# Edge loops of a graph attention kernel: the sum of gathered rows in two pieces, VectorE's steps in another order, GpSimd's turn signals out

## The chip, the cores and the metric

The kernel runs on one core of a Trainium2 chip. The metric is the device time of one launch in microseconds (us). TensorE (PE in the profile), VectorE (DVE), ScalarE (ACT), GpSimd (POOL) and SyncE (SP) run side by side, each through its own list of instructions, and order themselves by semaphores.

## What is computed

One layer of a graph transformer on 625 nodes of 768 features: two graph attention layers (GATv2) over 10,625 edges, a linear attention mixer, and a mixture of experts. The change touches the edge part of both attention layers:

```python
def gatv2(x, src, dst, Ws, bs, Wd, bd, attn):
    H, D = attn.shape                       # 8 x 96 in the first layer, 1 x 768 in the second
    fs = (x @ Ws + bs).reshape(-1, H, D)
    fd = (x @ Wd + bd).reshape(-1, H, D)
    e = leaky_relu(fs[src] + fd[dst], 0.2)
    logits = einsum('ehd,hd->eh', e, attn)
    m = segment_max(logits, dst)
    ex = exp(logits - m[dst])
    alpha = ex / segment_sum(ex, dst)[dst]
    return elu(segment_sum(alpha[:, :, None] * fs[src], dst))
```

The kernel writes the leaky relu as 0.2 z + 0.8 relu(z). The part 0.2 z is linear, so its product with `attn` is worked out once for each node and carried along in the last columns of the gathered rows (8 more columns in layer 1, one more in layer 2). What is left for each edge is the sum of two rows, max(z, 0) times the scaled attention vector, and a sum over each head.

## The kernel before

The edges lie in 84 tiles of 128 (one edge to a partition). Each of two loops ("loop 1", "loop 2") goes over the 84 tiles. A ring of G = 5 slots holds gathered rows. In the words used below:

- GpSimd issues three indirect transfers a step: the **source gather** (L577, rows of `table_src` into `ring_s`), the **target gather** (L583, rows of `table_dst` into `ring_d`) and the **scatter** (L588, the logits of a tile into a dense table). Step t waits until the logits of tile t are there (`edge_done`), gathers tile t+5 into the slot that came free, and scatters tile t. The three stand in one queue, in this order, and the first five tiles are gathered ahead of the loop. A step's scatter also waits for the scatter six tiles back.
- VectorE, in loop 1, does for tile t the **sum** of the two gathered rows (L1026, 776 columns, waits for both gathers), the **one-hot** rows of the tile ahead (L1033, used by TensorE to count edges in L1533), the **product** with the attention vector (L1038, 768 columns, both inputs in SBUF), the **head sums** (L1042) and the **total** (L1047, 8 columns, which signals `edge_done`). In the code the total of tile t-1 stands ahead of the sum of tile t; that is the place right behind its own head sums.
- In loop 2 the one head's sum is taken by the product itself (L1068, whose second input lies in PSUM), so there are only sum (769 columns), product and total (L1073). From tile 67 on, steps of other work (`project`) are mixed in: divisions, weights, transposed tiles, and the results of the products that TensorE runs at the end of the loop.
- `turn` (L1017) lets VectorE wait, ahead of the total of tile t-1, for a signal `edge_turn` that GpSimd gives in front of the gathers of step t-3.

Loop 1 is followed by a load of the dense table and the softmax (`dense(0)`), loop 2 by `dense(1)`; both wait for the last tiles, in loop 2 by way of the `project` steps.

Of the kernel before, what the change touches and what calls it, by code (L numbers as in the profile page):

```python
# [17 lines left out]
ALU = mybir.AluOpType  # L18
# [15 lines left out]
ET = -(-EDGES // EP)  # L34
FULL = EDGES // EP
SPREAD = 12
G = 5
# [12 lines left out]
DE_SLOTS = 8  # L50
PROJ_STEPS = 5 + 3 * T
PROJ_FROM = ET - PROJ_STEPS + 3
TURN_LAG = 3
TREE = N // 2
BL = CAP // 128

# [11 lines left out]
def build(nc, x, src, dst, W1s, b1s, W1d, b1d, attn1, ln1_w, ln1_b, Wos, bos, Wod, bod, attno, lno_w,  # L68
          lno_b, qkv_wT, qk_bcols, v_brow, proj_wT, proj_b, proj_matT, gate_wT, gate_bias, moe_w, out):
    ctx = ExitStack()  # L70
    with ctx:
        def sem(name):
            return ctx.enter_context(nc.semaphore(name))
# [10 lines left out]
        def dram(name, shape, dt=F32):  # L84
# [3 lines left out]
        WL = [DX, D + 1]  # L88
# [109 lines left out]
        ring_s, ring_d, hot_s, hot_d = zone([  # L198
            ("ring_s", [EP, G, DX], F32), ("ring_d", [EP, G, DX], F32),
            ("hot_s", [EP, G, TP], F16), ("hot_d", [EP, G, TP], F16)])  # L200
# [49 lines left out]
        z_ready, mul_ready = [sem(f"z_ready{l}") for l in range(2)], [sem(f"mul_ready{l}") for l in range(2)]  # L250
        sum_ready = sem("sum_ready")
        edge_done = [sem(f"edge_done{l}") for l in range(2)]
        edge_turn = [sem(f"edge_turn{l}") for l in range(2)]
        scattered = [sem(f"scattered{w}") for w in range(W)]
        hot_square, hot_d_ready = sem("hot_square"), sem("hot_d_ready")
        hot_ready, hot_used, counts_ready = sem("hot_ready"), sem("hot_used"), sem("counts_ready")
# [296 lines left out]
        def _(pool):  # L553
# [19 lines left out]
            def edges(l):  # L573

                def gather_src(t):
                    j = t % G
                    pool.indirect_dma_start(  # L577
                        out=ring_s[:, j, 0:WL[l]], out_offset=None, in_=table_src[l],
                        in_offset=bass.IndirectOffsetOnAxis(ap=src_i[:, t:t + 1], axis=0)).then_inc(gathered[j], 16)

                def gather_dst(t):
                    j = t % G
                    pool.indirect_dma_start(  # L583
                        out=ring_d[:, j, 0:WL[l]], out_offset=None, in_=table_dst[l],
                        in_offset=bass.IndirectOffsetOnAxis(ap=dst_i[:, t:t + 1], axis=0)).then_inc(gathered[j], 16)

                def scatter(t):
                    pool.indirect_dma_start(  # L588
                        out=dense_logits[l], out_offset=bass.IndirectOffsetOnAxis(ap=cell_i[:, t:t + 1], axis=0),
                        in_=logits[:, t, 0:HL[l]], in_offset=None).then_inc(scattered[t % W], 16)  # L590

                pool.wait_ge(idx_ready, 1)
                pool.wait_ge(src_written[l], TABLE)
                pool.wait_ge(mm_used, 20 * l + 15)
                for t in range(G):
                    gather_src(t)
                pool.wait_ge(mm_used, 20 * l + 20)
                pool.wait_ge(dst_written[l], TABLE + 16)
                for t in range(G):
                    gather_dst(t)  # L600
                pool.wait_ge(filled[l], 16)
                for t in range(ET):
                    pool.wait_ge(edge_done[l], t + 1)
                    if t + G < ET:
                        pool.sem_inc(edge_turn[l], 1)
                        gather_src(t + G)
                        gather_dst(t + G)
                    if t >= W:
                        pool.wait_ge(scattered[t % W], scatters(l, t - W))
                    scatter(t)  # L610
# [288 lines left out]
        def _(dve):  # L899
# [114 lines left out]
                dve.wait_ge(ext_ready, (2 * l + 2) * T)  # L1014
                dve.tensor_scalar((rows[:, 2, :], att_ps)[l], rows[:, 2, :], 0.8, None, ALU.mult).then_inc(att_scaled, 1)

            def turn(l, t):  # L1017

                if TURN_LAG <= t < ET - G + TURN_LAG:
                    dve.wait_ge(edge_turn[l], t - TURN_LAG + 1)  # L1020

            def edge_sum(l, t):

                j = t % G
                dve.wait_ge(gathered[j], gathers(l, t))
                dve.tensor_tensor(ring_s[:, j, 0:WL[l]], ring_s[:, j, 0:WL[l]], ring_d[:, j, 0:WL[l]], ALU.add).then_inc(z_ready[l], 1)  # L1026

            def edges_first():

                def hot(t):  # L1030
                    if t >= G:
                        dve.wait_ge(hot_used, t - G + 1)
                    dve.tensor_scalar(hot_s[:, t % G, :], iota_h[:, :], src_f[:, t:t + 1], None, ALU.is_equal).then_inc(hot_ready, 1)  # L1033

                def weigh(t):
                    dve.wait_ge(z_ready[0], t + 1)
                    v = ring_s[:, t % G, 0:D]
                    dve.scalar_tensor_tensor(out=v, in0=v, scalar=0.0, in1=rows[:, 2, :], op0=ALU.max, op1=ALU.mult).then_inc(mul_ready[0], 1)  # L1038

                def heads(t):  # L1040
                    dve.wait_ge(mul_ready[0], t + 1)
                    dve.tensor_reduce(head_sum[:, t % 2, :], ring_s[:, t % G, 0:D].rearrange("p (h d) -> p h d", h=HEADS1),  # L1042
                                      AX.X, ALU.add).then_inc(sum_ready, 1)

                def total(t):
                    dve.wait_ge(sum_ready, t + 1)
                    dve.tensor_tensor(logits[:, t, :], head_sum[:, t % 2, :], ring_s[:, t % G, D:DX], ALU.add).then_inc(edge_done[0], 1)  # L1047

                scale_attention(0)
                hot(0)  # L1050
                dve.wait_ge(att_scaled, 1)
                for t in range(ET):
                    turn(0, t)
                    if t >= 1:
                        total(t - 1)
                    edge_sum(0, t)
                    if t + 1 < ET:
                        hot(t + 1)
                    weigh(t)
                    heads(t)  # L1060
                total(ET - 1)

            def edges_second():

                def weigh(t):
                    dve.wait_ge(z_ready[1], t + 1)
                    j = t % G
                    dve.scalar_tensor_tensor(out=ring_d[:, j, 0:D], in0=ring_s[:, j, 0:D], scalar=0.0, in1=att_ps,  # L1068
                                             op0=ALU.max, op1=ALU.mult, accum_out=head_sum[:, t % 2, 0:1]).then_inc(mul_ready[1], 1)

                def total(t):
                    dve.wait_ge(mul_ready[1], t + 1)
                    dve.tensor_tensor(logits[:, t, 0:1], head_sum[:, t % 2, 0:1], ring_s[:, t % G, D:D + 1], ALU.add).then_inc(edge_done[1], 1)  # L1073

                scale_attention(1)
                dve.wait_ge(att_scaled, 2)
                for t in range(ET):
                    turn(1, t)
                    if t >= 1:
                        total(t - 1)  # L1080
                    edge_sum(1, t)
                    weigh(t)
                    if t >= PROJ_FROM:
                        project(t - PROJ_FROM)
                total(ET - 1)
                for i in range(ET - PROJ_FROM, PROJ_STEPS):
                    project(i)
# [773 lines left out]
```

## Time and profile before

| what | us |
|---|---|
| median of 3 runs | 1390.19 |
| lowest and highest of them | 1387.32, 1390.58 |
| the profiled execution, its own time | 1390.04 |
| its span | 1388.3 |
| loop 1, from GpSimd's first step to its last scatter | 103.59 to 434.84 |
| loop 2, the same | 650.73 to 991.50 |

The span is the stretch between the first and the last instruction of the profiled execution; 1.7 us of its own time lie around it. Two views matter for what follows. The groups of instructions by line say how often a line ran, how long one of it took and what ended the idle time ahead of it. The timeline lists single instructions by their start. A GpSimd row there is the issue of an indirect transfer, not its data; when the rows have landed is seen from the VectorE instruction that waits for them.

### The profile page before, as it was taken

The numbers are of one execution on the slowest core, as the hardware profiler recorded it, in microseconds if no ns is written. First come the engines' busy times: TensorE is split into PE (matmuls) and PEld (weight loads), VectorE is DVE, ScalarE is ACT, GpSimd is POOL, SyncE is SP. The second block draws the span as 40 slices with busy tenths as digits, with TensorE's granted clock in tenths as the row PEclk, the third lists the DMA queues.
The fourth block names the chain that finished last, engine by engine and source line by source line (L and its number), as shares of the span: only waits on it lengthen the run. The fifth ranks groups of instructions, "written<-read, shape, count | busy, mean of one in ns | idle before, by whom it ended". The sixth has DMA issues, their size and how long they took to land.

```text
span 1388.3 us, 16222 instructions
## 1 busy us (share of the span) xinstructions
PE 1039.6 (75%) x5539; PEld 859.2 (62%) x5539; DVE 946.6 (68%) x1650; ACT 563.7 (41%) x736; POOL 609.0 (44%) x581
## 2 busy tenths in 40 slices
PE   5974555555542688799999999607987998999981
PEld 5963333333321578797778787405755997888871
DVE  6649878877884798545554455564568665999993
ACT  3304333333331798300443333411054324777770
POOL 1037777777774000014777777787300000333330
PEclk9989777677785789899999999856987899999995
DMA  9956667666676850238777766858413026999986
GB/s 336 358 193 172 198 189 203 198 196 198 195 200 156 209 141 24 80 110 258 225 231 225 234 190 201 264 158 228 112 68 121 4 102 269 398 402 402 401 341 189
DMA packets 85035, 290.87 MB, mean 210 GB/s; under 512 B 15970, under 2 KB 37768, under 8 KB 84341
## 3 DMA queue, kind: packets, MB, share of 16 engines
q0 software_dynamic: 34656, 145.11, 34.9%
q1 hardware_dynamic: 46822, 130.71, 27.7%
q10 hardware_dynamic: 3488, 14.16, 2.6%
q8 instruction: 40, 0.66, 0.2%
q14 instruction: 29, 0.24, 0.1%
HBM read 258.31 MB, written 31.62 MB: 209 GB/s over the span
## 4 chain that ended last, share of the span: by engine, by line
PE 36%; DMA 16%; DVE 16%; POOL 15%; issue 14%; ACT 2%; SPq 0%; DVEq 0%; POOLq 0%; ACTq 0%
DMA ring_d<-table_dst,dst_i 12%; PE ps L1473 10%; PE ps L1474 10%; PE ps L1475 10%; POOL dense_logits L588 7%; POOL ring_s L577 4%; POOL ring_d L583 4%; DVE ring_s L1026 3%; PE ps L1570 2%; DVE head_sum L1042 2%; DVE ring_s L1038 1%; DVE ring_d L1068 1%; PE ps L1504 1%; PE ps L1554 1%; DMA dl_b<-dense_logits 1%
## 5 line engine op out<-in xcount | busy, mean ns | idle before, releaser
L577 POOL DMA_INDIRECT ring_s<-table_src,src_i x168 | 169.7, 1010 | 317.1 <-DVE fd_stage L950 257.0
L1533 PE MATMUL ps<-hot_s,hot_d 128*125 128x512 f16 (+1 forms) x840 | 180.2, 379 | 159.2 <-DVE hot_s L1033 159.2
L1026 DVE TENSOR_TENSOR ring_s<-ring_s,ring_d 128x776 f32<-128x776 f32 (+1 forms) x168 | 162.1, 965 | 195.3 <-DMA ring_d<-table_dst,dst_i 195.1
L1533 PEld LDWEIGHTS ps<-hot_s,hot_d 128*125 128x125 f16 x840 | 113.5, 175 | 226.1 <-DVE hot_s L1033 169.5
L588 POOL DMA_INDIRECT dense_logits<-logits,cell_i x168 | 201.6, 1200 | 55.2 <-issue 48.4
L583 POOL DMA_INDIRECT ring_d<-table_dst,dst_i x168 | 167.1, 995 | 76.4 <-issue 42.9
L705 ACT ACTIVATE hot_d<-iota_h,dst_bias 128x626 f16<-128x626 f16 x84 | 68.6, 816 | 218.1 <-PE ps L1533 218.1
L1473 PE MATMUL ps<-wp,at 128*125 128x384 f32 x300 | 107.2, 357 | 11.4 <-issue 4.4
L617 POOL COPY gather_i<-lst 128x1 int32 (+1 forms) x16 | 7.4, 464 | 238.3 <-DVE lst L1393 143.0
L1474 PE MATMUL ps<-wp,at 128*125 128x384 f32 x300 | 105.0, 350 | 0.0
L1475 PE MATMUL ps<-wp,at 128*125 128x384 f32 x300 | 104.8, 349 | 0.0
L1280 DVE TENSOR_TENSOR we<-eraw,we 128x1536 fp32r<-128x1536 f32 x50 | 86.4, 1756 | 12.8 <-ACT we L837 11.8
L1570 PE MATMUL ps<-fs,dpt 125*125 125x96 f32 (+1 forms) x500 | 89.9, 334 | 0.0
L1068 DVE SCALAR_TENSOR_TENSOR ring_d<-ring_s,ps 128x768 f32<-128x768 f32 x84 | 80.2, 954 | 2.9
L1042 DVE TENSOR_REDUCE head_sum<-ring_s 128x8 f32<-128x768 f32 x84 | 80.0, 953 | 2.9
L1610 PE MATMUL ps<-xt,mix_w 128*128 128x313 f32 (+1 forms) x288 | 80.3, 436 | 2.0 <-issue 1.7
L1570 PEld LDWEIGHTS ps<-fs,dpt 125*125 125x125 f32 x500 | 72.3, 208 | 13.1 <-issue 1.7
L1038 DVE SCALAR_TENSOR_TENSOR ring_s<-ring_s,rows 128x768 f32<-128x768 f32 x84 | 79.9, 951 | 0.0
L1280 DVE TENSOR_TENSOR we<-raw,we 128x1536 fp32r<-128x1536 f32 x44 | 75.8, 1751 | 0.0
L837 ACT CAST we<-eraw 128x1536 fp32r<-128x1536 f32 x50 | 72.2, 1480 | 5.6 <-PE ps L1475 5.6
L1610 PEld LDWEIGHTS ps<-xt,mix_w 128*128 128x128 f32 x288 | 54.5, 192 | 27.7 <-ACT mix_qp L792 5.2
L1473 PE MATMUL ps<-we,atg 128*128 128x512 f32 x168 | 68.0, 405 | 3.9 <-issue 1.9
(253 smaller groups left out, 2316.0 us busy)
## 6 DMA issues: line engine op xcount, KB each, us to landing
eraw<-in_moe_w_dram SPq DMA_DIRECT2D x50, 768.0 KB, 6.7
raw<-in_moe_w_dram SPq DMA_DIRECT2D x44, 768.0 KB, 7.1
dense_logits<-neg ACTq DMA_DIRECT2D x1, 12288.0 KB, 43.8
mix_w<-in_qkv_wT_dram SPq DMA_DIRECT2D x18, 384.0 KB, 6.3
dl_a<-dense_logits SPq DMA_DIRECT2D x2, 2187.5 KB
dl_b<-dense_logits SPq DMA_DIRECT2D x2, 2187.5 KB
y_in<-y_rows SPq DMA_DIRECT2D x5, 672.0 KB
ring_s<-table_src,src_i POOLq DMA_INDIRECT x168, 4.2
```

The lines of the kernel that those rows point to most:

```text
L577: pool.indirect_dma_start(out=ring_s[:, j, 0:WL[l]], out_offset=None, in_=table_src[l], in_offset=bass.IndirectOffsetOnAxis(ap=src_i[:, t: ...
L583: pool.indirect_dma_start(out=ring_d[:, j, 0:WL[l]], out_offset=None, in_=table_dst[l], in_offset=bass.IndirectOffsetOnAxis(ap=dst_i[:, t: ...
L588: pool.indirect_dma_start(out=dense_logits[l], out_offset=bass.IndirectOffsetOnAxis(ap=cell_i[:, t:t + 1], axis=0), in_=logits[:, t, 0:HL[ ...
L1026: dve.tensor_tensor(ring_s[:, j, 0:WL[l]], ring_s[:, j, 0:WL[l]], ring_d[:, j, 0:WL[l]], ALU.add).then_inc(z_ready[l], 1)
L1042: dve.tensor_reduce(head_sum[:, t % 2, :], ring_s[:, t % G, 0:D].rearrange("p (h d) -> p h d", h=HEADS1), AX.X, ALU.add).then_inc(sum_read ...
L1280: dve.tensor_tensor(we[:, 2 * m + 1, part], src, we[:, 2 * m, part].bitcast(F32), ALU.subtract).then_inc(up_lo if q < 4 else w2_lo, 1)
L1473: pe.matmul(o, lt(0), r(0), start=start, stop=False)
L1474: pe.matmul(o, lt(0), r(1), start=False, stop=False)
L1475: return pe.matmul(o, lt(1), r(0), start=False, stop=stop)
L1533: last = pe.matmul(ps[0:P, b, o:o + s1 - s0], hot_d[:, j, c * P:(c + 1) * P], hot_s[:, j, s0:s1], start=start and (n <= 5 or n == 9), stop ...
L1570: last = pe.matmul(o, pt[:, m * N + s * P:m * N + (s + 1) * P], fs[:, s, col:col + w], start=s == 0, stop=s == T - 1)
L1610: last = pe.matmul(ps[:, b, 0:c1 - c0], mix_w[:, 1 - m, k, s * 128:(s + 1) * 128], xt_v[:, k, c0:c1], start=k == 0, stop=k == KC - 1)
```

## The change

The sum is issued as two instructions, columns 0 to 527 and the rest (248 columns in loop 1, 241 in loop 2). In loop 1 VectorE's order within a tile becomes: the two pieces of the sum, the head sums of the tile one back, the product, the one-hot, the total of the tile one back. In loop 2 the total of the tile one back moves behind the sum. `turn` and GpSimd's signal go.

```diff
-TURN_LAG = 3
+SUM_AT = 528
...
                     if t + G < ET:
-                        pool.sem_inc(edge_turn[l], 1)
                         gather_src(t + G)
...
-            def turn(l, t):
-
-                if TURN_LAG <= t < ET - G + TURN_LAG:
-                    dve.wait_ge(edge_turn[l], t - TURN_LAG + 1)
-
             def edge_sum(l, t):
 
                 j = t % G
                 dve.wait_ge(gathered[j], gathers(l, t))
-                dve.tensor_tensor(ring_s[:, j, 0:WL[l]], ring_s[:, j, 0:WL[l]], ring_d[:, j, 0:WL[l]], ALU.add).then_inc(z_ready[l], 1)
+                for cols in (slice(0, SUM_AT), slice(SUM_AT, WL[l])):
+                    last = dve.tensor_tensor(ring_s[:, j, cols], ring_s[:, j, cols], ring_d[:, j, cols], ALU.add)
+                last.then_inc(z_ready[l], 1)
...
                 for t in range(ET):
-                    turn(0, t)
+                    edge_sum(0, t)
+                    if t >= 1:
+                        heads(t - 1)
+                    weigh(t)
+                    if t + 1 < ET:
+                        hot(t + 1)
                     if t >= 1:
                         total(t - 1)
-                    edge_sum(0, t)
-                    if t + 1 < ET:
-                        hot(t + 1)
-                    weigh(t)
-                    heads(t)
+                heads(ET - 1)
                 total(ET - 1)
...
                 for t in range(ET):
-                    turn(1, t)
+                    edge_sum(1, t)
                     if t >= 1:
                         total(t - 1)
-                    edge_sum(1, t)
                     weigh(t)
```

VectorE's list in the middle of loop 1, one tile and the start of the next; before:

```order
L1026 TENSOR_TENSOR ring_s<-ring_s,ring_d 128x776 [waits gathered2]
L1033 TENSOR_SCALAR hot_s<-iota_h,src_f 128x626 [waits hot_used]
L1038 SCALAR_TENSOR_TENSOR ring_s<-ring_s,rows 128x768 [waits z_ready0]
L1042 TENSOR_REDUCE head_sum<-ring_s 128x8 [waits mul_ready0]
L1047 TENSOR_TENSOR logits<-head_sum,ring_s 128x8 [waits sum_ready,edge_turn0]
L1026 TENSOR_TENSOR ring_s<-ring_s,ring_d 128x776 [waits gathered3]
```

and with the change (line numbers are 5 to 6 lower there):

```order
L1020 TENSOR_TENSOR ring_s<-ring_s,ring_d 128x528 [waits gathered0]
L1020 TENSOR_TENSOR ring_s<-ring_s,ring_d 128x248
L1037 TENSOR_REDUCE head_sum<-ring_s 128x8 [waits mul_ready0]
L1033 SCALAR_TENSOR_TENSOR ring_s<-ring_s,rows 128x768 [waits z_ready0]
L1028 TENSOR_SCALAR hot_s<-iota_h,src_f 128x626 [waits hot_used]
L1042 TENSOR_TENSOR logits<-head_sum,ring_s 128x8 [waits sum_ready]
L1020 TENSOR_TENSOR ring_s<-ring_s,ring_d 128x528 [waits gathered1]
```

The head sums, now of the tile one back, stand between the sum and the product; the product starts one instruction later and the total leaves its place ahead of the next sum's wait.

VectorE's list in loop 2, two tiles; before:

```order
L1026 TENSOR_TENSOR ring_s<-ring_s,ring_d 128x769 [waits gathered0]
L1068 SCALAR_TENSOR_TENSOR ring_d,head_sum<-ring_s,ps 128x768 [waits z_ready1]
L1073 TENSOR_TENSOR logits<-head_sum,ring_s 128x1 [waits mul_ready1,edge_turn1]
L1026 TENSOR_TENSOR ring_s<-ring_s,ring_d 128x769 [waits gathered1]
L1068 SCALAR_TENSOR_TENSOR ring_d,head_sum<-ring_s,ps 128x768 [waits z_ready1]
```

and with the change:

```order
L1020 TENSOR_TENSOR ring_s<-ring_s,ring_d 128x528 [waits gathered0]
L1020 TENSOR_TENSOR ring_s<-ring_s,ring_d 128x241
L1069 TENSOR_TENSOR logits<-head_sum,ring_s 128x1 [waits mul_ready1]
L1064 SCALAR_TENSOR_TENSOR ring_d,head_sum<-ring_s,ps 128x768 [waits z_ready1]
L1020 TENSOR_TENSOR ring_s<-ring_s,ring_d 128x528 [waits gathered1]
```

The total sits between sum and product of the next tile. GpSimd's list of transfers keeps its order.

## Rows read from the trace of the kernel before

**Rows 1.** The page's first part: busy us of each engine (share of the span), instructions.

```profile
PE 1039.6 (75%) x5539; PEld 859.2 (62%) x5539; DVE 946.6 (68%) x1650; ACT 563.7 (41%) x736; POOL 609.0 (44%) x581
```

**Rows 2.** Groups by line, middle of loop 1 (127.8 to 427.0): POOL, then DVE.

```profile
L588 POOL DMA_INDIRECT dense_logits<-logits,cell_i x74 | 91.5, 1237 | 22.5 <-issue 22.5
L577 POOL DMA_INDIRECT ring_s<-table_src,src_i x74 | 71.8, 970 | 22.5 <-issue 22.5
...
L1026 DVE TENSOR_TENSOR ring_s<-ring_s,ring_d 128x776 f32<-128x776 f32 x74 | 71.6, 967 | 50.1 <-DMA ring_d<-table_dst,dst_i 49.9
L1042 DVE TENSOR_REDUCE head_sum<-ring_s 128x8 f32<-128x768 f32 x74 | 70.5, 953 | 2.5
L1038 DVE SCALAR_TENSOR_TENSOR ring_s<-ring_s,rows 128x768 f32<-128x768 f32 x74 | 70.3, 951 | 0.0
```

**Rows 3.** Timeline, loop 1, POOL (start, us, engine, line, tiles).

```profile
308.12 0.95 POOL L583 DMA_INDIRECT ring_d<-table_dst,dst_i  x1 [0.30 <-issue]
309.37 0.98 POOL L588 DMA_INDIRECT dense_logits<-logits,cell_i  x1 [0.30 <-issue]
...
313.17 1.44 POOL L588 DMA_INDIRECT dense_logits<-logits,cell_i  x1 [0.30 <-issue]
314.92 0.97 POOL L577 DMA_INDIRECT ring_s<-table_src,src_i  x1 [0.30 <-issue]
```

**Rows 4.** Timeline of the same stretch, DVE.

```profile
308.52 0.97 DVE L1026 TENSOR_TENSOR ring_s<-ring_s,ring_d 128x776 f32<-128x776 f32 x1 [0.41 <-DMA ring_d<-table_dst,dst_i]
309.41 0.38 DVE L1033 TENSOR_SCALAR hot_s<-iota_h,src_f 128x626 f16<-128x626 f16 x1
...
311.75 0.17 DVE L1047 TENSOR_TENSOR logits<-head_sum,ring_s 128x8 f32<-128x8 f32 x1
312.80 0.97 DVE L1026 TENSOR_TENSOR ring_s<-ring_s,ring_d 128x776 f32<-128x776 f32 x1 [0.88 <-DMA ring_d<-table_dst,dst_i]
```

**Rows 5.** Timeline, the one transfer that started within a product: DVE, then POOL.

```profile
203.62 0.94 DVE L1038 SCALAR_TENSOR_TENSOR ring_s<-ring_s,rows 128x768 f32<-128x768 f32 x1
...
203.66 1.76 POOL L588 DMA_INDIRECT dense_logits<-logits,cell_i  x1 [0.30 <-issue]
```

**Rows 6.** Timeline, two additions back to back (DVE) and a transfer within the first (POOL).

```profile
915.07 1.82 DVE L1091 TENSOR_TENSOR b<-mix_out,mix_rden 125x768 f32<-125x768 f32 x2
...
915.63 1.24 POOL L577 DMA_INDIRECT ring_s<-table_src,src_i  x1 [0.30 <-issue]
```

**Rows 7.** Timeline, source gathers just behind a sum's start: two DVE and POOL pairs.

```profile
112.55 0.96 DVE L1026 TENSOR_TENSOR ring_s<-ring_s,ring_d 128x776 f32<-128x776 f32 x1
112.62 1.72 POOL L577 DMA_INDIRECT ring_s<-table_src,src_i  x1 [0.30 <-issue]
...
957.84 1.03 DVE L1026 TENSOR_TENSOR ring_s<-ring_s,ring_d 128x769 f32<-128x769 f32 x1 [3.35 <-DMA ring_d<-table_dst,dst_i]
...
957.87 0.97 POOL L577 DMA_INDIRECT ring_s<-table_src,src_i  x1 [0.30 <-issue]
```

**Rows 8.** Groups by line, POOL, loop 2 ahead of the projection (650.7 to 908).

```profile
L588 POOL DMA_INDIRECT dense_logits<-logits,cell_i x63 | 71.9, 1141 | 19.2 <-issue 18.3 <-DVE logits L1073 0.9
L577 POOL DMA_INDIRECT ring_s<-table_src,src_i x64 | 65.2, 1019 | 23.6 <-issue 21.8 <-DVE logits L1073 1.8
L583 POOL DMA_INDIRECT ring_d<-table_dst,dst_i x63 | 62.3, 989 | 19.2 <-issue 17.7 <-DVE logits L1073 1.5
```

**Rows 9.** Timeline, starts of both loops: POOL's first step, and DVE's second sum in loop 2.

```profile
103.59 0.94 POOL L577 DMA_INDIRECT ring_s<-table_src,src_i  x1 [2.31 <-issue]
...
650.56 0.96 DVE L1026 TENSOR_TENSOR ring_s<-ring_s,ring_d 128x769 f32<-128x769 f32 x1 [0.61 <-DMA ring_d<-table_dst,dst_i]
...
650.73 1.61 POOL L577 DMA_INDIRECT ring_s<-table_src,src_i  x1 [4.40 <-issue]
```

**Rows 10.** The chain that ended last, behind loop 1 and at loop 2's end.

```profile
433.88 2.09 DMA dense_logits<-logits,cell_i
...
951.10 1.48 PE ps L1491 x6
```

More of the change, by code:

```diff
@@ L252, in build @@
         edge_done = [sem(f"edge_done{l}") for l in range(2)]
-        edge_turn = [sem(f"edge_turn{l}") for l in range(2)]
         scattered = [sem(f"scattered{w}") for w in range(W)]
```

## Prediction, made before the changed kernel was run

> **What bounds the kernel now.** GpSimd is busy for only 44% of the span [rows 1], so the share of busy time does not show it as a bound; it has to be read stage by stage. I went first to the groups by line for the middle of loop 1. There each of GpSimd's three transfers has the same idle time ahead of it, 22.5 us over 74 of them, or 0.30 us each, and "issue" as its cause [rows 2]: it waits for nobody. VectorE's sum on the other hand sits idle for 50.1 us in the same stretch, and the rows of the target gather end nearly all of it [rows 2]. So GpSimd's list of transfers sets the pace of loop 1 and VectorE follows it. 74 steps in 299.2 us are 4.04 us a step.
>
> What is in those 4.04 us: the unheld transfers take 0.98 (scatter), 0.97 (source gather) and 0.95 us (target gather), and three idle times of 0.30 make 3.80 [rows 2, 3]. The rest is in the scatter, which takes 1.237 us in the mean [rows 2]. The timelines show when: a scatter that starts at 313.17 us, 0.37 behind the start of the sum at 312.80, takes 1.44 us, and one that starts 0.85 behind it takes 0.98 [rows 3, 4]. The hold (0.46 us) ends at 313.63, 0.14 ahead of the end of the sum. The same holds for a source gather 0.07 behind a sum's start (1.72 for 0.97, up to 0.14 ahead of the sum's end) [rows 7]. I read it so: a transfer whose issue starts within a sum waits until about 0.13 us ahead of the sum's end; once a transfer has begun, a sum that starts later does not stretch it (the target gather at 308.12 keeps its 0.95 although the sum starts at 308.52) [rows 3, 4].
>
> **The rhythm.** The target gather that ends at 309.07 is followed by its sum at 312.80, 3.73 us later [rows 3, 4]; over the 74 tiles this lag lies between 3.36 and 4.02, with a spread of 0.13. Call x the start of the scatter, counted from the start of the sum it meets. As the scatter starts 0.30 behind the end of its target gather, the next x is the step less 3.43. Before the change: x = 0.37 gives a hold up to 0.84, a step of 4.27; then x = 0.84, no hold, 3.80; then 0.37 again. The mean is 4.04, as measured, so I trust the rule.
>
> **The change, part by part.**
>
> *Splitting the sum.* 776 columns take 0.97 and 8 take 0.17 us [rows 4], so 528 take 0.71 and 248 take 0.42. The next instruction starts 0.08 ahead of the end of one that it doesn't depend on (one-hot at 309.41, sum until 309.49) [rows 4]; the second piece runs from 0.63 to 1.04. Does a waiting transfer get in between the pieces? Two additions of 0.95 ran back to back from 915.07, and the source gather at 915.63 took 1.24, held by 0.27 up to 915.90, which is 0.12 ahead of the end of the first [rows 6]. So yes. A transfer is held until 0.58 in the first piece and until 0.91 in the second. For VectorE the second instruction costs 0.07 us a tile, which costs nothing: it is hidden by its wait for rows, 0.68 us a tile [rows 2].
>
> *Loop 2.* The product there has an input in PSUM and holds nobody; 63 steps took 257.3 us, 4.08 each. Holds: 0.16 on the scatter, 0.05 on the source gather, 0.04 on the target gather over their unheld lengths [rows 8], 0.25 in all. With the pieces the rhythm is x = 0.37 (hold to 0.58, step 4.01), x = 0.58 (3.80): 3.91, and about 3.95 when the spread carries some scatters into the second piece. Gain 0.10 us a step. It counts up to tile 76, whose transposes let TensorE begin its row of products at 951.10 on the chain [rows 10]; from there on TensorE sets the end. 75 steps: -7.5 us. The total of the first tile now waits for the second tile's sum (at 650.56, in pieces until 651.5), so GpSimd starts at about 652.5 where it was 650.73 [rows 9]: +1.8. Loop 2: **-6 us**.
>
> *The order in loop 1.* The head sums (0.95) stand where the one-hot stood, so the product, which ran from 1.18 to 2.13 behind the sum's start, now runs from 1.83 to 2.78. This is what decides the case. In the middle of loop 1 no source gather started within a product: they start 1.28 behind the release of the scatter, at 2.12 or later, as the product ends, and take 0.97 us in the mean [rows 2]. The trace of loop 1 has one transfer that did start in a product: the scatter at 203.66, 0.04 behind its start, took 1.76, held to 0.12 ahead of the product's end [rows 5]. The product holds just as the sum does. The Trainium skill ("SBUF — State Buffer", section "Who interferes with whom") says that a VectorE instruction with two SBUF inputs contends with a GpSimd instruction that reads SBUF, and that one with at most one SBUF input, and a `tensor_reduce`, doesn't; by that rule moving the reduction ahead of the product moves a hold, and the one row agrees. By the section's other remark, marked as inferred there, that additions don't stall descriptor generation, neither would hold and the split would be worth nothing; the held scatter [rows 3, 4] contradicts it.
>
> With the change the product holds from 1.83 to 2.65. Three cases for a step:
> (A) x below 0.58: the scatter is released at 0.58, the source gather starts at 1.86. That is 0.03 behind the product's start, and whether it is held there the trace leaves open: 0.03 behind a sum it was not held (957.87), 0.07 behind it was (112.62) [rows 7]. Step 4.38 - x if it is free, 0.79 more if it is held.
> (B) x from 0.63 to 0.91: released at 0.91, source gather at 2.19, held by 0.46. Step 3.80 + (0.91 - x) + 0.46.
> (C) x above 0.91: the source gather starts at x + 1.28 and is held by 1.37 - x. Step 5.17 - x.
> The next x is again the step less 3.43. If the source gather is free in A, there are two rhythms: A after A (0.37, 0.58) at 3.91 us a step, and B, C, B (0.75, 0.99) at 4.30. The second x of the fast one lies at the edge of B, and a spread of 0.13 throws it over in every second pair; from the slow one it takes a lag some 0.17 beyond the mean to get back. I put a third of the steps in the fast rhythm: 4.17. If A is held, x goes 0.37, 1.37, 0.37 (4.80, 3.80), or falls into B and C: 4.30 to 4.35 all along. The bounds are 3.91 and 4.35; I take 4.20, near the first case with some of the second: +0.16 over 79 steps with gathers, +12.6 us.
>
> *The edges of loop 1.* The first total now stands behind the second tile's sum, the head sums, the product and the one-hot, 2.6 us later than before, and GpSimd, which began its first step at 103.59 [rows 9] and has no slack afterwards, is later by as much. At the end VectorE has head sums and a total of two tiles behind the last sum: +1.1 us ahead of the scatter at 433.88, from which the chain goes on [rows 10]. In the first five steps GpSimd lost more than later (24.2 us, for 4.04 each 20.2), because VectorE's rhythm then is its own (3.3 us a tile); the pieces give some 2 us back. Loop 1: 12.6 + 2.6 + 1.1 - 2 = **+14.3 us**.
>
> *The later total.* Slot and logits are free one tile later. The total of tile t comes 3.0 us behind the sum of tile t+1; the gather into the slot is due about 15 us behind the sum of tile t, against 7 now needed. Cost nothing; without that slack it would be the whole delay.
>
> *The signals.* `turn` never binds: the total follows the head sums within 0.1 us in every tile of loop 1 (the extra wait is 0.07 of it, and lies on VectorE, beside its wait for rows), and GpSimd's idle time ahead of a source gather is the 0.30 of the others [rows 2]. Both go at nothing; bounds +-1 us.
>
> **Sum.** Against the profiled execution, span 1388.3 and 1.7 around it, 1390.0: +14.3 - 6 gives 1398.3; the median of 1390.19 lies 0.2 above it. I predict **1399 us**.
>
> **The rivals.**
> *Held in case A as well* (the source gather loses the race by 0.03 us, or a waiting transfer doesn't get in between the pieces): 4.33 a step, +23 for 12.6, so 1409. For it: the scatter at 203.66 was held 0.04 behind a product. Against it: 957.87 was not, 0.03 behind a sum. Chance 0.22.
> *It evens out*: the fast rhythm holds for most of the steps (4.05), loop 1 costs 3 us, loop 2 gives 5: 1388 to 1393. It needs a spread half of that read, or starts of the source gather 0.05 earlier. 0.15.
> *Faster*: the product doesn't hold a source gather. Only one row says that it does, and that was a scatter, with a one-hot ending just then. Then loop 1 has loop 2's rhythm, 3.95: -0.09 x 79, with the edges -5.4, with loop 2 -11.5: 1378.5. It decides from the first source gather that starts at 2.19 and takes 0.97. For it speaks that the rhythm of holds is calm otherwise; against it, that the hold in that row ends at the same 0.12 ahead of the end. 0.15.
> *The change's steps fall where I say*: 1394 to 1405. 0.48.
>
> **How the numbers follow.** The range takes in the forecast, the held case and the evening out: 1386 to 1412, which leaves out the faster case and a little beyond either end. Within 0.3% (4.2 us, about what a measurement of this kernel can tell from no change) is the third case and the low edge of the first: 0.16. Faster 0.17, slower 0.67.
>
> **What would show it.** In the middle of loop 1 of the changed kernel: the source gather's mean rises from 0.97 to 1.2 to 1.3 us, the scatter's falls from 1.24 to 1.06 or so, and source gathers of 1.43 us (held by 0.46) are the most frequent held ones. A step of 4.2. In loop 2 the scatter's mean falls from 1.14 to about 1.07 and the step by 0.1. The forecast is wrong if source gathers within the product take 0.97, if the lag of 3.73 changes, or if GpSimd waits for logits in the middle of the loop.

## The result

The changed kernel took 1407.37 us in the median of 4 runs (1401.02 to 1413.06), the kernel before 1390.38 beside it (1387.32 to 1391.30): ratio 1.0134, 95% interval 1.0105 to 1.0162. It is slower, as forecast, and by twice the 9 us forecast: 17 to 19 us. Timed once more, in a set of its own beside the kernel before, it took 1406.45 us (1402.22 to 1410.0), ratio 1.0126 (1.0097 to 1.0154). The kernel before spreads by 4 us in the first set and the changed one by 12; in the second set both spread by 8.

The profiled execution of the changed kernel is its slowest, 1413.06 us with a span of 1411.3. Busy times of the two loops, from the first target gather to the end of the last scatter, show where the time went (columns: stretch, its length, then busy us of PE, its weight loads, DVE, ACT and POOL with counts, granted clock, DMA share, GB/s). Before:

```profile
95.00:434.90 339.90, 177.87 (x836) 112.10 (x834) 272.14 (x419) 126.44 (x169) 262.79 (x247) 0.77 0.67 194
640.30:991.60 351.30, 292.00 (x1583) 229.18 (x1582) 190.45 (x356) 109.06 (x237) 264.67 (x247) 0.90 0.73 215
```

After:

```profile
94.40:467.90 373.50, 191.57 (x830) 119.29 (x830) 262.89 (x503) 125.70 (x169) 293.35 (x247) 0.71 0.62 176
673.40:1013.80 340.40, 292.38 (x1582) 229.84 (x1581) 186.68 (x440) 108.95 (x237) 253.03 (x247) 0.91 0.74 222
```

Loop 1 is 33.6 us longer, loop 2 10.9 shorter, and the 205.5 us between the loops are the same. GpSimd's 247 transfers take 30.6 us more in loop 1 and 11.6 less in loop 2: nearly the whole of the first difference and all of the second is time within transfers. In the changed kernel the source gather is L576, the target gather L582 and the scatter L587. The middle of loop 1 (130 to 455), group by group, and below it the target gather of the kernel before:

```profile
L576 POOL DMA_INDIRECT ring_s<-table_src,src_i x72 | 93.5, 1298 | 21.9 <-issue 21.9
L587 POOL DMA_INDIRECT dense_logits<-logits,cell_i x73 | 89.8, 1231 | 22.2 <-issue 22.2
L582 POOL DMA_INDIRECT ring_d<-table_dst,dst_i x73 | 77.1, 1056 | 22.2 <-issue 22.2
...
L583 POOL DMA_INDIRECT ring_d<-table_dst,dst_i x74 | 70.0, 945 | 22.5 <-issue 16.8 <-DVE logits L1047 5.8
```

Beside [rows 2] the source gather went from 970 to 1298 ns and the target gather from 945 to 1056, while the scatter kept its 1.23 us. The idle time is 0.30 us ahead of each, as before: GpSimd still waits for nobody. ("Held" means that the issue took longer than these unheld lengths, "free" that it didn't.) In loop 2 (683.7 to 940) the scatter fell from 1141 ns [rows 8] to 1083, the target gather from 989 to 960:

```profile
L587 POOL DMA_INDIRECT dense_logits<-logits,cell_i x65 | 70.4, 1083 | 19.8 <-issue 19.8
...
L582 POOL DMA_INDIRECT ring_d<-table_dst,dst_i x65 | 62.4, 960 | 19.8 <-issue 19.8
```

Single steps of loop 1 show two places. The first, POOL and then DVE:

```profile
143.22 1.01 POOL L587 DMA_INDIRECT dense_logits<-logits,cell_i  x1 [0.30 <-issue]
144.54 1.74 POOL L576 DMA_INDIRECT ring_s<-table_src,src_i  x1 [0.30 <-issue]
...
142.68 1.03 DVE L1020 TENSOR_TENSOR ring_s<-ring_s,ring_d 128x528 f32<-128x528 f32 x2 [1.48 <-DMA ring_d<-table_dst,dst_i]
...
144.49 0.95 DVE L1033 SCALAR_TENSOR_TENSOR ring_s<-ring_s,rows 128x768 f32<-128x768 f32 x1
```

The source gather starts 1.86 us behind the sum (142.68) and 0.05 behind the product (144.49), and is held for 0.77 us, up to 0.13 ahead of the product's end. That is case A of the prediction, decided against the free gather. The second place was in none of its cases:

```profile
163.92 1.37 POOL L582 DMA_INDIRECT ring_d<-table_dst,dst_i  x1 [0.30 <-issue]
165.60 1.78 POOL L587 DMA_INDIRECT dense_logits<-logits,cell_i  x1 [0.30 <-issue]
167.68 0.97 POOL L576 DMA_INDIRECT ring_s<-table_src,src_i  x1 [0.30 <-issue]
168.96 1.25 POOL L582 DMA_INDIRECT ring_d<-table_dst,dst_i  x1 [0.30 <-issue]
170.51 1.78 POOL L587 DMA_INDIRECT dense_logits<-logits,cell_i  x1 [0.30 <-issue]
...
163.76 1.04 DVE L1020 TENSOR_TENSOR ring_s<-ring_s,ring_d 128x528 f32<-128x528 f32 x2 [0.62 <-DMA ring_d<-table_dst,dst_i]
...
165.58 0.95 DVE L1033 SCALAR_TENSOR_TENSOR ring_s<-ring_s,rows 128x768 f32<-128x768 f32 x1
...
168.68 1.04 DVE L1020 TENSOR_TENSOR ring_s<-ring_s,ring_d 128x528 f32<-128x528 f32 x2 [1.78 <-DMA ring_d<-table_dst,dst_i]
```

A target gather that starts within the first piece of the sum (at 163.92) is let go at 0.58 behind the sum's start (163.76). The scatter behind it then starts at 1.83, a hair behind the product (165.60 against 165.58), and is held for 0.80. The source gather starts at 3.92, free, and the next target gather (168.96) falls 0.28 into the next sum. So the pattern comes again: 4.9 us a step. I call it the locked rhythm. Of 73 steps in the middle of loop 1, counted from source gather to source gather, 20 took more than 4.75 us in this profile and 6 in the second one of the same kernel, whose loop 1 took 364.9 us and loop 2 343.1. The mean step was 4.50 in the first and 4.38 in the second, for 4.06 before.

### The profile page after: what moved, and what is told of

It is laid out like the page before. It is cut to its first block, busy times and chain, and to the rows that moved or that the text cites. A ratio compares the mean times of both kernels' runs of the same rounds, so it can differ in the third digit from the quotient of the medians.

```text
span 1411.3 us, 16076 instructions
## 1 busy us (share of the span) xinstructions
PE 1054.1 (75%) x5539; PEld 867.6 (61%) x5539; DVE 933.4 (66%) x1818; ACT 563.5 (40%) x736; POOL 627.0 (44%) x581
## 4 chain that ended last, share of the span: by engine, by line
PE 36%; POOL 34%; issue 12%; DVE 9%; DMA 7%; ACT 2%; SPq 0%; DVEq 0%; POOLq 0%; ACTq 0%
POOL ring_s L576 12%; POOL dense_logits L587 12%; POOL ring_d L582 10%; PE ps L1468 10%; PE ps L1469 10%; PE ps L1470 10%; DMA ring_d<-table_dst,dst_i 3%; PE ps L1565 2%; PE ps L1499 1%; PE ps L1549 1%; DMA y_in<-y_rows 1%; DMA dl_b<-dense_logits 1%; DMA dl_a<-dense_logits 1%; DVE tree L1128 1%; DVE ring_s L1020 1%
## 5 line engine op out<-in xcount | busy, mean ns | idle before, releaser
L1020 DVE TENSOR_TENSOR ring_s<-ring_s,ring_d 128x528 f32<-128x528 f32 x336 | 173.7, 558 | 251.4 <-DMA ring_d<-table_dst,dst_i 251.4
L576 POOL DMA_INDIRECT ring_s<-table_src,src_i x168 | 194.0, 1155 | 318.5 <-DVE fd_stage L948 256.3
L1528 PE MATMUL ps<-hot_s,hot_d 128*125 128x512 f16 (+1 forms) x840 | 193.1, 399 | 180.5 <-DVE hot_s L1028 180.3
L1528 PEld LDWEIGHTS ps<-hot_s,hot_d 128*125 128x125 f16 x840 | 120.3, 185 | 253.4 <-DVE hot_s L1028 191.1
L587 POOL DMA_INDIRECT dense_logits<-logits,cell_i x168 | 191.6, 1141 | 57.0 <-issue 50.0
L582 POOL DMA_INDIRECT ring_d<-table_dst,dst_i x168 | 171.7, 1022 | 76.5 <-issue 50.6
```

The source lines that it names most:

```text
L576: pool.indirect_dma_start(out=ring_s[:, j, 0:WL[l]], out_offset=None, in_=table_src[l], in_offset=bass.IndirectOffsetOnAxis(ap=src_i[:, t: ...
L582: pool.indirect_dma_start(out=ring_d[:, j, 0:WL[l]], out_offset=None, in_=table_dst[l], in_offset=bass.IndirectOffsetOnAxis(ap=dst_i[:, t: ...
L587: pool.indirect_dma_start(out=dense_logits[l], out_offset=bass.IndirectOffsetOnAxis(ap=cell_i[:, t:t + 1], axis=0), in_=logits[:, t, 0:HL[ ...
L1020: last = dve.tensor_tensor(ring_s[:, j, cols], ring_s[:, j, cols], ring_d[:, j, cols], ALU.add)
L1528: last = pe.matmul(ps[0:P, b, o:o + s1 - s0], hot_d[:, j, c * P:(c + 1) * P], hot_s[:, j, s0:s1], start=start and (n <= 5 or n == 9), stop ...
```

## The experiments

Loop 1 and loop 2 are, in each profile, from the first target gather to the end of the last scatter. Times in us; ratios against the kernel before, timed beside it. The two kernels marked * leave out a part of the work (see below). The loops and the step are from one profile each.

| kernel | median | ratio (95%) | loop 1 | loop 2 | mean step, loop 1 |
|---|---|---|---|---|---|
| before | 1390.4 | | 339.8 | 351.1 | 4.06 |
| changed | 1407.4 | 1.0134 (1.0105 to 1.0162) | 373.4 | 340.3 | 4.50 |
| changed, again | 1406.5 | 1.0126 (1.0097 to 1.0154) | 364.9 | 343.1 | 4.38 |
| split only | 1378.5 | 0.9910 (0.9883 to 0.9938) | 335.9 | 341.2 | 4.05 |
| order (and signals out), no split | 1414.3 | 1.0161 (1.0108 to 1.0214) | 363.1 | 353.4 | 4.37 |
| signals out only | 1387.6 | 0.9977 (0.9955 to 0.9999) | 340.9 | 350.8 | 4.08 |
| changed, product from PSUM * | 1375.7 | 0.9898 (0.9847 to 0.9949) | 331.5 | 343.3 | 3.94 |
| split, old order, product from PSUM * | 1371.3 | 0.9889 (0.9868 to 0.9910) | 328.3 | 343.2 | 3.95 |
| changed, cut at 464 | 1388.8 | 1.0001 (0.9984 to 1.0018) | 350.6 | 343.4 | 4.20 |
| changed, cut at 496 | 1395.6 | 1.0051 (1.0032 to 1.0069) | 356.6 | 342.8 | 4.29 |
| changed, cut at 512 | 1400.7 | 1.0088 (1.0055 to 1.0121) | 358.7 | 341.2 | 4.30 |
| split, product mostly from PSUM | 1369.9 | 0.9875 (0.9856 to 0.9894) | 327.7 | 340.9 | 3.94 |
| the same, sum in three pieces | 1362.4 | 0.9811 (0.9784 to 0.9838) | 325.9 | 336.0 | 3.92 |

The theory going in: VectorE instructions with both inputs in SBUF hold GpSimd's transfers, the split shortens the holds, and the new order puts the product where the source gather starts. The rivals: the split itself costs (S), the lost signals cost (T), the later totals or the longer list cost (L).

**The edits one by one.** Split only, on the kernel before:

```diff
+SUM_AT = 528
...
-                dve.tensor_tensor(ring_s[:, j, 0:WL[l]], ring_s[:, j, 0:WL[l]], ring_d[:, j, 0:WL[l]], ALU.add).then_inc(z_ready[l], 1)
+                for cols in (slice(0, SUM_AT), slice(SUM_AT, WL[l])):
+                    last = dve.tensor_tensor(ring_s[:, j, cols], ring_s[:, j, cols], ring_d[:, j, cols], ALU.add)
+                last.then_inc(z_ready[l], 1)
```

> The kernel before with nothing but the sum split at column 528 (order of VectorE's steps, totals and turn signals as before). Theory H (VectorE instructions with both inputs in SBUF hold GpSimd's transfers; the loss lies in where the product stands): both loops gain; loop 1 by 3 to 5 us (scatter's mean in its middle 1.24 to about 1.12 us, some source gathers held by the product), loop 2 by 8 to 10; 1376 to 1380 in all. Rival S (the loss comes from the second sum instruction, or a waiting transfer does not get in between the pieces): 1390 or slower, with the scatter's mean at 1.24 or more.

It is 0.9% faster, with 3.9 us in loop 1 and 9.9 in loop 2. S is out for this order of steps. The groups in the middle of its loop 1 (scatter, then source gather):

```profile
L589 POOL DMA_INDIRECT dense_logits<-logits,cell_i x69 | 75.8, 1098 | 21.0 <-issue 20.4 <-DVE logits L1050 0.6
L578 POOL DMA_INDIRECT ring_s<-table_src,src_i x69 | 74.8, 1084 | 21.0 <-issue 20.7 <-DVE logits L1050 0.3
```

The scatter lost 0.14 us of its 1.237 [rows 2], but the source gather, free before at 970, now takes 1084: let go earlier, it starts within the product, which runs from 1.25 to 2.20 us behind the sum's start in this order. So the split gives less in loop 1 than in loop 2, where the product holds nobody; with the product of loop 1 reading PSUM as well, further down, loop 1 gains 11.5 us and not 3.9.

The order: the changed kernel with the sum in one instruction again. Its signals are out too, and its totals later; the next run takes out the signals by themselves.

```diff
-                for cols in (slice(0, SUM_AT), slice(SUM_AT, WL[l])):
-                    last = dve.tensor_tensor(ring_s[:, j, cols], ring_s[:, j, cols], ring_d[:, j, cols], ALU.add)
-                last.then_inc(z_ready[l], 1)
+                dve.tensor_tensor(ring_s[:, j, 0:WL[l]], ring_s[:, j, 0:WL[l]], ring_d[:, j, 0:WL[l]], ALU.add).then_inc(z_ready[l], 1)
```

> The changed kernel with the sum in one instruction again (the new order of loop 1, the later totals, no signals). Theory H: the product runs from 1.75 to 2.7 us behind the sum's start, the source gather starts at 2.12 and is held by 0.45 us in most steps; loop 1 is 18 to 25 us longer than before, loop 2 within 3: 1408 to 1417. Rival S (the split is to blame): 1390 to 1394.

It is 1.6% slower; loop 1 is longer by 23.3 us, loop 2 by 2.3. Most of the loss belongs to the order. But the two edits don't simply add: the split, which gives 3.9 us in loop 1 in the old order, takes 1.8 and 10.3 us more there in the new one (364.9 and 373.4 us against 363.1). The places where that goes are the two shown above.

Signals out only:

```diff
-                        pool.sem_inc(edge_turn[l], 1)
...
-                    turn(0, t)
...
-                    turn(1, t)
```

> The kernel before without GpSimd's signals and VectorE's waits for them. Theory H: no wait of it ever binds, so within 2 us of before, the steps of both loops as before (4.06 and 4.14 us). Rival T (the signals kept a rhythm that the change lost): slower by 5 us or more, with source gathers held in loop 1.

Within 0.3%, at or a little below the kernel before (the median is 1.7 us lower). T is out; whether the signals cost some 2 us or nothing, this set can hardly tell.

**Does the product hold the gathers?** The changed kernel with the attention vector of loop 1 in PSUM. To make room for it, this kernel leaves out the tenth of the ten matmuls that count a tile's edges, so a part of its counts is missing; TensorE also has less to do. The kernel at the end of this section keeps all its counts and takes that doubt away:

```diff
-                dve.tensor_scalar((rows[:, 2, :], att_ps)[l], rows[:, 2, :], 0.8, None, ALU.mult).then_inc(att_scaled, 1)
+                dve.tensor_scalar(att_ps, rows[:, 2, :], 0.8, None, ALU.mult).then_inc(att_scaled, 1)
...
-                    dve.scalar_tensor_tensor(out=v, in0=v, scalar=0.0, in1=rows[:, 2, :], op0=ALU.max, op1=ALU.mult).then_inc(mul_ready[0], 1)
+                    dve.scalar_tensor_tensor(out=v, in0=v, scalar=0.0, in1=att_ps, op0=ALU.max, op1=ALU.mult).then_inc(mul_ready[0], 1)
...
-                for n, (b, o, s0, s1) in enumerate(cbanks):
+                for n, (b, o, s0, s1) in enumerate(cbanks[:9]):
```

> The changed kernel, but the product of loop 1 reads the attention vector from PSUM, as loop 2's does; its bank is made free by leaving out the tenth counting matmul of each tile (113 columns of the last count tile, so the result is not the reference's there; PE is not on the path). Theory H: the product no longer holds anyone, the source gather takes 0.97 in the middle of loop 1 although it starts in the product, loop 1 is 34 to 42 us shorter than in the changed kernel's profile, 5 to 9 shorter than before: 1374 to 1380. Rival L (the later totals or VectorE's own list are to blame): loop 1 stays at 4.4 to 4.5 us a step, 1400 or more.

Some 31 us faster than the change, 1.0% faster than before. Loop 1 fell from 373.4 to 331.5 with VectorE's list and its totals where the change put them, so L is out. One source gather (POOL) and its product (DVE):

```profile
202.30 0.97 POOL L576 DMA_INDIRECT ring_s<-table_src,src_i  x1 [0.31 <-issue]
...
202.25 0.94 DVE L1033 SCALAR_TENSOR_TENSOR ring_s<-ring_s,ps 128x768 f32<-128x768 f32 x1
```

The source gather starts 0.05 us behind the product, the very place at which it was held for 0.77 us in the changed kernel, and takes 0.97; so do all 56 source gathers of this loop 1 that start there. The instruction is of the same kind and length; only its second input moved from SBUF to PSUM. The Trainium skill ("SBUF — State Buffer", section "Who interferes with whom") says that a VectorE instruction with two SBUF inputs contends with a GpSimd instruction that reads SBUF, and that one with at most one SBUF input, outside the two-port modes, doesn't. The trace agrees for the product: 0.77 us against nothing. The section's remark, marked as inferred, that additions don't stall descriptor generation does not hold here: with the product free, scatters in the sum are still held (1104 ns in the mean for 976).

The prediction told the second half of that rule without its condition, and the experiments' expectations name only sum and product as holding. The trace of the kernel before has a third instruction that holds, though it has one SBUF input, the one-hot. DVE, then POOL:

```profile
325.66 0.38 DVE L1033 TENSOR_SCALAR hot_s<-iota_h,src_f 128x626 f16<-128x626 f16 x1
...
325.75 1.13 POOL L588 DMA_INDIRECT dense_logits<-logits,cell_i  x1 [0.30 <-issue]
```

This scatter is held by 0.16 us, up to 0.13 ahead of the one-hot's end, and seven more of the same loop by 0.06 to 0.13. It is short and so costs little, but it is not free.

The same product in the old order, with the split:

> Split sum in the old order of steps (with the turn signals), and the product of loop 1 reading the attention vector from PSUM; as in the run with that product in the new order, the tenth counting matmul of each tile is left out to free the bank. Theory H: only the two pieces of the sum hold GpSimd; loop 1 from its first target gather to its last scatter takes 329 to 331 us (before 339.8, changed kernel 373.4), loop 2 341 to 343; 1368 to 1373. Rival L (the new order itself is worth something once the product is free): the same as the new order's 1375.7 or slower.

1371.3 against 1375.7, timed in different sets, with intervals of the ratio that overlap: the new order has nothing to give once the product is free. In the profiles the middle step is the same (3.95 and 3.94), and what the new order costs is at the edges; loop 1 takes 328.3 for 331.5.

**How close was the race?** The changed kernel with one number changed:

```diff
-SUM_AT = 528
+SUM_AT = 464
```

> The changed kernel with the sum cut at column 464 instead of 528. A scatter held by the first piece is then let go 0.07 us earlier, and its source gather starts at 1.79 us, 0.03 ahead of the product's start at 1.83, where it was 0.03 behind it. Theory H with a race for the start: these source gathers are free, the rhythm in which the scatter itself starts at 1.83 in the product is gone; loop 1 takes 350 to 355 us (step 4.15 to 4.25), 1391 to 1397. Rival N (only the mean place of the product counts, 0.07 us change nothing): 1405 to 1411 as the changed kernel.

Loop 1 took 350.6 us as expected; the whole, at 1388.8, fell below the range expected and is even with the kernel before. 64 columns, 0.07 us of a hold, are worth 18 us. The mean step of loop 1, 4.20, is the very one that the prediction had put into its sum for a case A that is mostly free; yet this kernel took 1388.8 and not 1399. The two cuts in between:

> The changed kernel with the sum cut at column 496. The source gather behind a scatter let go by the first piece then starts within 0.01 us of the product's start (528: 0.03 behind, held; 464: 0.03 ahead, free). Theory H with a race: some or all of these source gathers are held for 0.8 us, loop 1 between the 350.6 us of 464 and the 365 to 373 of 528, without the rhythm in which the scatter is held at 1.83; 1392 to 1405. Rival G (the time falls evenly with the length of the first piece): 1396 to 1400, half way.

> The changed kernel cut at column 512, source gather 0.015 us behind the product's start. Theory H with a race: all of these gathers held as at 528 (0.8 us each), 1399 to 1408. Rival G (evenly with the length): 1400 to 1403 as well, but with shorter holds of the source gather instead of fewer free ones.

Cut at 496, the source gather starts so near to the product's start that it wins one time and loses the next. Two POOL and DVE pairs of that kernel:

```profile
205.08 0.97 POOL L576 DMA_INDIRECT ring_s<-table_src,src_i  x1 [0.30 <-issue]
209.29 1.78 POOL L576 DMA_INDIRECT ring_s<-table_src,src_i  x1 [0.30 <-issue]
...
205.07 1.00 DVE L1033 SCALAR_TENSOR_TENSOR ring_s<-ring_s,rows 128x768 f32<-128x768 f32 x1
209.27 0.95 DVE L1033 SCALAR_TENSOR_TENSOR ring_s<-ring_s,rows 128x768 f32<-128x768 f32 x1
```

Where it wins, the product takes 0.05 us longer (1.00 for 0.95). Read to the nanosecond, all source gathers of loop 1 that start near the product's start:

| cut | start behind the product's | free | held about 0.8 us |
|---|---|---|---|
| 464 | -21 to -14 ns | all 15 | 0 |
| 496 | 13 to 18 ns | 8 | 7 |
| 512 | 29 to 35 ns | 0 | all 10 |
| 528 (both profiles) | 45 to 51 ns | 0 | all 33 |

The scatters of the locked rhythm at cut 528 say the same: in the first profile those 10 to 14 ns behind the product's start were free (5), those 15 ns and more behind were held (19). The race tips between 13 and 17 ns behind the start. Rival G, an even slope, gets the times of 512 and 496 about right but not their mechanism: what changes from 464 to 512 is the count of gathers that lose, and each that loses is held in full. From 512 to 528 the scatters of the locked rhythm change sides: at 512 four scatters started 0 to 4 ns behind the product's start and were free.

**A kernel that beats both.** Only one PSUM bank is free in loop 1, 512 of the 768 columns. So the product goes in two pieces, first the 256 columns that hold, at a place where no transfer starts, then 512 from PSUM; split sum, old order, no signals:

```diff
+                    dve.tensor_scalar(ps[:, 7, :], rows[:, 2, 0:512], 0.8, None, ALU.mult)
...
-                    v = ring_s[:, t % G, 0:D]
-                    dve.scalar_tensor_tensor(out=v, in0=v, scalar=0.0, in1=rows[:, 2, :], op0=ALU.max, op1=ALU.mult).then_inc(mul_ready[0], 1)
+                    v, w = ring_s[:, t % G, 0:512], ring_s[:, t % G, 512:D]
+                    dve.scalar_tensor_tensor(out=w, in0=w, scalar=0.0, in1=rows[:, 2, 512:D], op0=ALU.max, op1=ALU.mult)
+                    dve.scalar_tensor_tensor(out=v, in0=v, scalar=0.0, in1=ps[:, 7, :], op0=ALU.max, op1=ALU.mult).then_inc(mul_ready[0], 1)
```

> A whole kernel: before, with the split sum, without the signals, and with loop 1's product in two pieces: first its last 256 columns with the attention vector in SBUF (behind the sum's start 1.25 to 1.67 us, no transfer starts there), then 512 columns with the vector in the one free PSUM bank, which hold nobody. Theory H: source gathers at 1.86 and 2.19 us meet only the second piece, so loop 1 as with the whole product in PSUM, 329 to 332 us; 1368 to 1375, faster than both kernels. Rival S (a further instruction in VectorE's list costs time): 1378 or more.

1369.9 us, 1.25% faster than before, as fast as with the whole product in PSUM, and with all the counts. In its loop 1, 62 transfers started well within the piece that reads PSUM, and none was held. With the sum in three pieces on top:

```diff
-                for cols in (slice(0, SUM_AT), slice(SUM_AT, WL[l])):
+                for cols in (slice(0, 264), slice(264, 528), slice(528, WL[l])):
```

> The kernel with the split sum, no signals and loop 1's product mostly from PSUM, its sum now in three pieces (264, 264 and the rest). Theory H: no hold of a transfer by the sum is longer than 0.35 us; each loop gains another 2 to 4 us; 1363 to 1368. Rival S (each further instruction costs its 0.07 us on the path): 1369 to 1375.

1362.4 us, 1.9% faster than before and a little below what was expected; most of it came in loop 2 (-4.9 us, and -1.8 in loop 1). VectorE's busy time is 974.5 us over the whole kernel, for 946.6 before. In the middle of loop 1 its sums still sit idle for 23.9 us (50.1 before [rows 2]), nearly all of it until rows land, and GpSimd waits for nobody (scatter, source gather, target gather):

```profile
L589 POOL DMA_INDIRECT dense_logits<-logits,cell_i x70 | 75.0, 1071 | 21.3 <-issue 21.3
L578 POOL DMA_INDIRECT ring_s<-table_src,src_i x70 | 68.5, 978 | 21.3 <-issue 21.3
L584 POOL DMA_INDIRECT ring_d<-table_dst,dst_i x71 | 67.5, 951 | 21.6 <-issue 21.6
```

## Why the prediction was half right

**The bound and the rule of the hold** were right. GpSimd's list sets the pace in the middle of loop 1 in every kernel here (idle 0.30 us ahead of each transfer), and of loop 2 but for a few steps, and "held until 0.13 us ahead of the end" fits them: of the 1836 transfers of both loops in the 13 profiles that took over 0.06 us longer than unheld, all but one were let go within 0.03 us of that point of a sum, a product, a one-hot or one of two instructions of the other work.

**The split** was right: a waiting transfer gets in between the pieces, and loop 2 gained. The size was a little low. Forecast -7.5 for the steps and +1.8 for the start, -6; measured -10.9 and -8.0 in the two profiles of the change, -9.9 with the split alone. Over the first 63 steps of loop 2, those that the prediction had measured, the step fell by the 0.10 assumed; over the 75 that it counted, with other work mixed in at their end, by 0.13 to 0.14. GpSimd's first step came 0.05 us earlier in one profile and 1.1 later in the other, not 1.8 later.

**The product holds** was right, on the strength of one row [rows 5]; the product from PSUM shows it.

**The step that failed** is the mean step of loop 1, taken at 4.20 us and measured at 4.50 and 4.38. Two errors stand behind it. The first is case A. I left its race open, with the source gather 0.03 behind the product's start, and leaned to "free", because a gather 0.03 behind the start of a sum had been free [rows 7]. It was held every time. The start was 45 to 51 ns behind, and the product wins from some 15 ns on, so it would have been held at 0.03 as well. The row of a sum was the wrong one to compare with. One difference is that this sum came after a wait for its rows while the product follows directly on the head sums; that this is the reason is not shown. The row nearest in kind was the held scatter 0.04 behind a product [rows 5], which I had put on the rival's side. The rival "held in case A as well" said 4.33 a step and 1409; the median was 1407.4. That it comes so near is in part luck: the step was above 4.33 in both profiles (4.38, 4.50), and loop 2 gave back 8 to 11 us where the sum had 6. The same luck is in the forecast: with case A free (cut at 464) the step was 4.20 and the time 1388.8, so that for the case it leaned to, the 1399 was some 10 us too high. In that kernel's profile loop 1 was 10.8 us longer than before, for 14.3 in the sum, and loop 2 7.7 shorter, for 6.

The second error: the list of cases lets only scatter and source gather be held, never the target gather. For the held case A it says "x goes 0.37, 1.37, 0.37 (4.80, 3.80)". But by its own figures the next sum starts 3.73 behind the end of a target gather, and the next target gather starts 0.95 ahead of its own end, so after a step of more than 4.68 us the target gather falls into the next sum, after one of 4.80 by 0.12. It is held until 0.58, and the scatter behind it starts at 1.83, in the product, and not at 1.37. Of the cases only a held A makes a step so long, and each entry into the locked rhythm behind the first steps of loop 1, in both profiles, came from a source gather that was held at the product's start. What keeps it going is one of the signs named beforehand: by a lag of 3.73 the target gather after a step with x = 1.83 would start 0.08 ahead of the next sum and be free, but behind a held target gather the lag was 3.49 and 3.42 in the mean (3.77 and 3.76 behind the others). Why the rows come sooner there, no run tells.

The scatter started at that place in 24 of 73 steps of the first profile and in 9 of the second. These steps took 4.99 and 5.07 us in the mean, the others 4.26 and 4.29. So the locked rhythm takes 17.5 and 7.1 us of loop 1, which puts the step above 4.33 and makes up the 8.4 us between the two profiles.

**The edges**: GpSimd's first step of loop 1 came 10.6 and 10.8 us behind the first target gather for 8.5 before, +2.0 and +2.3 for the 2.6 forecast. The first five steps took 22.6 and 22.2 us for 24.3 (-2 forecast), and the stretch behind the last source gather was 1.4 and 1.7 us longer (+1.1 forecast). **The signals** at nothing: right as far as one can tell; the run without them was 1.7 us faster (1387.6 against 1389.3), with an interval that reaches from nothing to 6 us, so the bound of 1 us is not shown.

So the sum of the parts was 14.3 - 6. Measured, in the first profile: 33.6 in loop 1, -10.9 in loop 2, -0.6 ahead of loop 1 and 0.8 behind loop 2, which makes up the 23.0 between the spans. In the second profile, which lies nearer to the median: 25.2 and -8.0, and behind the last scatter, where TensorE's products and not the scatter set the end, another 3.4.

The signs named beforehand: the source gather's mean at 1.2 to 1.3 us was 1.30 (1.36 in the second profile); the scatter's, forecast to fall to 1.06, was 1.23 in the first profile and 1.11 in the second, and the locked rhythm, with its held scatters, makes most of the difference. Holds of 0.46 (1.40 to 1.43 us) were the most frequent ones in the second profile, 28 against 16 of 0.77; in the first there were 16 of them and 17 of 0.77.

## What to carry to other kernels

Where GpSimd's indirect transfers set the pace, look first for VectorE instructions with both inputs in SBUF, which were in their way here (the one-hot, with one input, held too, but briefly), and cut them short or move one of their inputs to PSUM; the number of further instructions is free as long as VectorE waits anyway. Reordering VectorE's work moves such an instruction onto another transfer, and as the hold is all or nothing, tens of nanoseconds decide over a per cent of the kernel. When you list the phases of such a rhythm, go once round the whole step with every transfer in it, also past the last phase that the trace before has shown.

## What the runs showed of the hardware

A transfer's issue that started up to 13 ns behind the start of a product that followed directly on another VectorE instruction still went first; from 17 ns on it was held for nearly all of it, and in between it went either way. Behind a sum that had waited for its rows, 36 ns were still free in the one case there is [rows 7]; why the two differ, no run here tells. The product that loses such a race by a hair took 0.05 us longer (1.00 for 0.95), while GpSimd in the same place loses 0.8. Transfers that started within a head sum or within a product that reads PSUM were free (at most 0.01 us longer, but for one of 0.07); those that started within a sum, a product with both inputs in SBUF or a one-hot, later than such a race and more than 0.13 us ahead of its end, were held until that point.
